# The second head's probabilities scaled on ScalarE instead of VectorE, in an attention loop of 128 steps

## What is computed

```python
def _gqa(q, k, v):
    scale = 1.0 / np.sqrt(q.shape[-1])
    scores = jnp.einsum('bsghd,btgd->bghst', q, k) * scale
    p = jax.nn.softmax(scores, axis=-1)
    return jnp.einsum('bghst,btgd->bsghd', p, v)
...
core = _gqa(q, k, v).reshape(b, s, nh * d)
qx = _fp8_linear_pertensor(ln_out, wqx, wqx_scale, qx_in_scale).reshape(b, s, g, hpg, d)
...
xout = _gqa(qx, kx, vx).reshape(b, s, nh * d)
cat = jnp.concatenate([core, xout], axis=-1)
catq = _div_clamp_fp8(cat, proj_smooth)
return jnp.einsum('bsi,oi->bso', catq, wproj) * (proj_in_scale * proj_w_scale)
```

## Time and profile before

| | |
|---|---|
| median of three runs | 1796.29 us (1796.28 to 1796.57) |
| profiled execution, its own time | 1798.47 us |
| its span | 1796.4 us |
| TensorE busy | 1741.4 us, 97% |
| VectorE busy | 1409.3 us, 78% |
| ScalarE busy | 1102.0 us, 61% |
| line 1244 (the scaling, 128x512) | 256 times, 124.5 us, 486 ns each |
| line 1002 (the exponential) | 256 times, 174.3 us, 689 ns each |

### The profile page before, as it was taken

How to read it: one execution, slowest core, us unless ns; L and a number is a source line. 1 busy time by engine, 2 the same in 40 slices (tenths; PEclk the granted TensorE clock), 3 DMA queues, 4 the chain that set the end, 5 groups by cost and what they waited for, 6 DMA issues and landing times.

```text
span 1796.4 us, 31332 instructions
## 1 busy us (share of the span) xinstructions
PE 1741.4 (97%) x10664; PEld 1186.5 (66%) x10664; DVE 1409.3 (78%) x4581; ACT 1102.0 (61%) x2378; POOL 272.0 (15%) x428
## 2 busy tenths in 40 slices
PE   9999999988999999999999999999999999989998
PEld 4444445666777776777777777777777777654554
DVE  1243526689888997888998889899889988979996
ACT  1131415376777775667677667777667766657776
POOL 0000000211111211111121111111112112201111
PEclk9999999999999999999999999999999999999999
DMA  7000000101312230121012012111210112000000
GB/s 270 24 0 24 0 0 25 37 1 52 105 48 85 71 95 3 55 73 36 26 48 73 24 50 73 36 36 39 75 41 19 61 54 95 3 1 19 24 24 30
DMA packets 45596, 83.30 MB, mean 46 GB/s; under 512 B 3584, under 2 KB 22528, under 8 KB 45056
## 3 DMA queue, kind: packets, MB, share of 16 engines
q1 hardware_dynamic: 45440, 81.31, 13.8%
HBM read 69.77 MB, written 10.49 MB: 45 GB/s over the span
## 4 chain that ended last, share of the span: by engine, by line
PE 68%; DVE 15%; issue 10%; ACT 4%; POOL 2%; DMA 0%; POOLq 0%; ACTq 0%
PE bank L536 15%; PE bank L645 8%; PE bank L599 7%; PE bank L694 6%; PE bank L623 4%; PE bank L730 3%; PE bank L410 3%; PE bank L496 3%; PE bank L470 3%; PE bank L458 3%; PE bank L488 3%; PE bank L578 3%; DVE nq L1234 2%; PE bank L437 2%; DVE nmx L1380 2%
## 5 line engine op out<-in xcount | busy, mean ns | idle before, releaser
L536 PE MATMUL bank<-wqs,XQ 128*128 128x256 f16 x2048 | 245.9, 274 | 4.6 <-DVE x L1265 4.6
L599 PE MATMUL bank<-prT,KV 128*128 128x256 f32 x1024 | 246.9, 384 | 0.0
L645 PE MATMUL bank<-kT,qT 128*128 128x512 f32 x512 | 242.2, 595 | 0.9 <-issue 0.9
L599 PEld LDWEIGHTS bank<-prT,KV 128*128 128x128 f32 x1024 | 190.5, 191 | 73.2 <-issue 52.2
L536 PEld LDWEIGHTS bank<-wqs,XQ 128*128 128x128 bf16 x2048 | 198.9, 99 | 43.6 <-DVE x L1265 11.4
L1002 ACT ACTIVATE pr<-bank,nmx 128x512 f32<-128x512 f32 x256 | 174.3, 689 | 42.7 <-DVE nmx L1380 41.4
L1549 POOL TENSOR_TENSOR rdev<-gvar,cst 128x7 f32<-128x7 f32 x128 | 191.0, 1492 | 10.0
L1547 POOL TENSOR_TENSOR gvar<-mvB,geps 128x7 f32<-128x7 f32 x128 | 30.8, 241 | 1061.4 <-DVE mvB L1224 1053.9
L1380 DVE TENSOR_REDUCE nmx<-bank 128x1 f32<-128x512 f32 x256 | 169.4, 683 | 12.0 <-PE bank L645 7.9
L694 PE MATMUL bank<-identf,pr 128*128 128x128 f32 x1024 | 153.7, 278 | 24.9 <-DVE pr L1244 20.1
L813 ACT ACTIVATE prT<-bank 128x512 f32<-128x512 f32 x256 | 153.2, 614 | 21.6 <-PE bank L694 21.4
(11 more groups left out here) (179 smaller groups left out, 3102.0 us busy)
## 6 DMA issues: line engine op xcount, KB each, us to landing
wa<-in_wgu SPq DMA_DIRECT2D x32, 512.0 KB, 3.7
wst<-in_wcat SPq DMA_DIRECT2D x21, 512.0 KB, 4.1
wpst<-in_wproj SPq DMA_DIRECT2D x8, 1024.0 KB, 6.4
wa<-in_wdn SPq DMA_DIRECT2D x16, 512.0 KB, 3.7
xT<-in_xT SPq DMA_DIRECT2D x4, 1024.0 KB, 6.9
wkx<-in_wkvx SPq DMA_DIRECT2D x8, 512.0 KB, 5.3
tern_gu<-wa SPq DMA_DIRECT2D x16, 256.0 KB, 2.0
wgu<-tern_gu SPq DMA_DIRECT2D x2, 2048.0 KB, 7.4
```

The costliest lines, as they stand in the source:

```text
L536: ins = mm(dst, XQ[:, b, c, k, j * P:(j + 1) * P], w, start=(k == 0 and m == 0), stop=(k == KT - 1 and m == 1))
L599: ins = mm(OB[:, 0:2 * P], KV[:, n % 2, t, P:2 * P], prT[:, st % 2, t, :, :].rearrange("p h s -> p (h s)"), start=(t == 0), stop=(t == ST ...
L645: mm(SB_[h][:], qT[:, h, st * P:(st + 1) * P], kT[:, :], start=True, stop=True).then_inc(s["scores_made"], 1)
```

## The change

In `scale_rows` VectorE takes both reciprocals, but multiplies only head 0. The second reciprocal signals a new semaphore, `ri_ready`; ScalarE waits for it and multiplies head 1 by it with an activation, in place, after `raw_kv` and `cross_out` and ahead of `ob_out`; it signals `pr1_scaled`, on which TensorE's turning of head 1 waits. The scaling of head 0 now comes after the wait for the second exponential and after the second reciprocal. The second reciprocal also waits until ScalarE's scaling of the step before is done, since that reads the same column of `ri`.

```diff
@@ TensorE, in pair
                     for h in range(2):
-                        pe.wait_ge(s["pr_scaled"], 2 * T + h + 1)
+                        pe.wait_ge(s["pr1_scaled" if h else "pr_scaled"], T + 1)
@@ ScalarE, in pair
                     if st == 1 and n > 1:
                         cross_out(n)
+                    act.wait_ge(s["ri_ready"], T + 1)
+                    act_f(pr[:, 1, :], pr[:, 1, :], ACT.Copy, scale=ri[:, 1:2]).then_inc(s["pr1_scaled"], 1)
                     if T:
                         ob_out(T - 1)
@@ VectorE
             def scale_rows(T, st):
 
-                for h in range(2):
-                    dve.wait_ge(s["exp_done"], 2 * T + h + 1)
-                    own.do(v.reciprocal(ri[:, h:h + 1], su[:, st, h:h + 1]))
-                    own.sync()
-                    v.tensor_scalar(pr[:, h, :], pr[:, h, :], ri[:, h:h + 1], None, ALU.mult).then_inc(s["pr_scaled"], 1)
+                dve.wait_ge(s["exp_done"], 2 * T + 1)
+                own.do(v.reciprocal(ri[:, 0:1], su[:, st, 0:1]))
+                dve.wait_ge(s["exp_done"], 2 * T + 2)
+                if T:
+                    dve.wait_ge(s["pr1_scaled"], T)
+                v.reciprocal(ri[:, 1:2], su[:, st, 1:2]).then_inc(s["ri_ready"], 1)
+                own.sync()
+                v.tensor_scalar(pr[:, 0, :], pr[:, 0, :], ri[:, 0:1], None, ALU.mult).then_inc(s["pr_scaled"], 1)
```

More of the change, by code:

```diff
@@ L222, in build @@
             max_ready exp_done raw_out kv_out kvx_out qt_out kt_out kxt_out ob_out pt_out pxt_out xexp_done
-            bn_ready stats_ready nq_ready pr_scaled xs_sub px_scaled cq_ready acc_done
+            bn_ready stats_ready nq_ready pr_scaled ri_ready pr1_scaled xs_sub px_scaled cq_ready acc_done
             wh_ready wl_ready wp_ready vx_copied cross_made cross_out
```

## The result

The changed kernel takes 1816.12 us (median of 4; 1815.76 to 1817.30), the kernel before in the same sitting 1796.43 us (1796.28 to 1798.17). The ratio is 1.0109, 95% interval 1.0091 to 1.0126: 19.7 us more. The forecast was 1815.7 us.

What follows compares the result with a forecast made beforehand. TensorE, 97% busy, bounds the kernel, losing time mainly at line 694 waiting for VectorE's scaling in first steps. Terms 9.2 + 1.3 + 3.5 + 5.4 = 19.4 us, added to the median, gave 1815.7 us; range 1803 to 1832.

Steps and rivals of the forecast that it cites:

- Kind A: 14 of 32 first steps, where exponentials are late: head 0 ready 0.66 us later with TensorE already waiting, 9.2 us.
- The last two steps: Last two steps of the loop, exponentials late too: head 0 ready 0.66 us later in each, 1.3 us.
- Second step: Second step of each pair: head 1, scaled on ScalarE, reaches TensorE 0.11 us late, 32 times, 3.5 us.
- Kind B: Other 18 first steps, exponentials ready and VectorE itself late: 0.3 us more each, 5.4 us.
- the carry: Rounding's net lateness from second to fourth steps into the next first step: 0.6 us, 0.2 after VectorE's waits for scores.
- my own sign of being wrong: Forecast fails if late first steps do not move, or second-step lateness reaches TensorE elsewhere than line 694.
- Rival 1: Fourth step's 0.43 us relief reaches first steps, 18 of which gain 0.33 us each: 1804.4 us, chance 0.14.
- rival 2: VectorE's relief reaches ScalarE's exponentials, which come 0.93 us earlier in 14 first steps: faster, 1783.5 us, chance 0.09.
- Rival 4: Over the whole loop, losses and relief cancel, with the second exponential hidden: 1796 us, chance 0.05.
- Rival 3: ScalarE's queue becomes the path, its added 0.63 us delaying the exponentials of 14 first steps: 1831.7 us, chance 0.12.

Runs made afterwards that it cites:

- e9_fourth_step: Against the kernel before, only the fourth step of each pair scales its second head on ScalarE, in the change's order: 1793.34 us, ratio 0.9981.
- e7_second_and_third: Against the kernel before, only the second and third steps of each pair scale their second head on ScalarE, in the change's order: 1813.77 us, ratio 1.0095.
- e1_reciprocals_first: Against the kernel before, VectorE takes both reciprocals first but still scales both heads; nothing moves to ScalarE: 1812.63 us, ratio 1.0079.
- e8_reciprocals_first_behind: Changed kernel with ScalarE's scaling behind the copy of the attended rows in first and third steps: 1813.46 us, ratio 1.0092 to the kernel before.

## Why the forecast held, point by point

*Kind A, 9.2 us.* Right in place and mechanism, a little too large. Here is the step of the earlier trace rows in the changed kernel, 7 us later:

```profile
956.16 0.16 DVE L1247 RECIPROCAL ri<-su 128x1 f32<-128x1 f32 x1 [0.50 <-ACT pr L1002]
956.24 0.47 DVE L1249 TENSOR_SCALAR pr<-pr,ri 128x512 f32<-128x512 f32 x1
956.36 0.72 ACT L1012 ACTIVATE pr<-pr,ri 128x512 f32<-128x512 f32 x1 [0.23 <-DVE ri L1247]
956.77 0.66 PE L694 MATMUL bank<-identf,pr 128*128 128x128 f32 x4 [2.01 <-DVE pr L1249]
956.99 0.61 ACT L979 ACTIVATE yb<-bank,rsT 128x128 bf16<-128x128 f32 x2
957.63 0.29 DVE L1256 TENSOR_SCALAR yb<-yb 128x512 bf16<-128x512 bf16 x1 [0.91 <-ACT yb L979]
```

VectorE idles 0.50 us for the second exponential, TensorE 2.01 us in place of 1.49. Eleven of the 13 steps cost 0.52 or 0.53 each and two 0.32 and 0.45, not 0.66: the scaling follows the second reciprocal by 0.08 us, since it waits only for the first. Sum 6.5 us. Line 694 starts 1.27 us after the first reciprocal; I had 1.4.

*The last two steps, 1.3 us.* The last but one costs 0.53 (in the table it is among the third steps), the last 1.11: 1.6 together, about right in size. Of the 1.11, 0.53 is what e9_fourth_step shows for this step, where only fourth steps have the new order; the other 0.58 is no part of my mechanism, since the last step takes 0.57 us more in e7_second_and_third too, where it is left as before; what makes it stays open.

*Second step, 3.5 us.* Right: 4.3 us. In a pair with even b (step 57):

```profile
930.58 1.27 ACT L987 ACTIVATE yb<-bank,rsT 128x512 bf16<-128x512 f32 x2
931.72 0.74 ACT L1012 ACTIVATE pr<-pr,ri 128x512 f32<-128x512 f32 x1
932.33 0.64 ACT L979 ACTIVATE yb<-bank,rsT 128x128 bf16<-128x128 f32 x2
```

```profile
931.42 0.63 PE L694 MATMUL bank<-identf,pr 128*128 128x128 f32 x4
931.88 0.60 PE L578 MATMUL bank<-identf,nq 128*128 128x128 f32 x4
932.51 0.66 PE L694 MATMUL bank<-identf,pr 128*128 128x128 f32 x4
```

Head 1 is scaled at 932.46 and turned at 932.51, where 0.44 us after line 578 would have been 932.32. It is 0.25 us a step with even b and 0.05 with odd b. The scaling holds the queue for 0.61 us (931.72 to 932.33; I had 0.63). The Trainium skill, page "ScalarE: Activation LUTs", section "What ACT_TABLE_LOAD costs", has figures that give 0.613 us as an estimate (706 ns less 93 ns of overlap), and the trace agrees. Rounding starts 3.58 us after the reciprocal; I had 3.7.

*Kind B, 5.4 us from the carry.* The size came out, the place did not. The delays of rounding were about right (+0.51, +0.44, and 2.03 us after the reciprocal in the fourth step, where I had 1.95), and I let them travel to the next first step, with a third of them lost in waits for scores. In the changed kernel they did not get there. The first instruction behind rounding that TensorE needs is the accumulation, and the fourth step's projections need it before. VectorE and TensorE of the changed kernel at step 55:

```profile
905.40 0.75 DVE L1270 SCALAR_TENSOR_TENSOR x<-bank,pscale,x 128x512 f32<-128x512 f32 x1
906.07 1.28 DVE L1385 TENSOR_REDUCE nmx<-bank 128x1 f32<-128x512 f32 x2
```

```profile
904.68 1.45 PE L645 MATMUL bank<-kT,qT 128*128 128x512 f32 x3
906.21 1.92 PE L536 MATMUL bank<-wqs,XQ 128*128 128x256 f16 x16
```

The accumulation ends at 906.15 and the projections begin at 906.21. Before, it ran from 898.97 to 899.72 and they began at 900.25, straight after the scores. There 5.4 us are lost, and kind B is 0.05 us shorter each. That my kind B gave 5.4 us too is chance. The failed step is the sentence that lateness is taken up by "VectorE's waits for scores"; I had looked for what VectorE waits for, and not for who waits for VectorE on the way. By my own sign of being wrong, "if lateness in the second step reaches TensorE in other places than line 694", the mechanism of this term is refuted: it reaches line 536, in the fourth step, once the third step's lateness is added (0.00 with the second step alone, 0.22 with both).

*Not in the sum at all:* the fall of the clock after a longer pause (1.67 us once in the trace), and 1.8 us in the first nine steps. So that 19.4 us came so near to 19.7 is in part luck: kind A was too large by 2.7 us, 5.4 us were put in the wrong place, and these two were missing.

*Two readings of the rows.* The 58.4 us of the earlier trace rows count one wait twice: all 18 waits on the matmul row are among the 37 on the weight-load row, at the same steps, and TensorE's matmuls stood 20.1 us for this reason, not 58. (On the two rows the changed kernel has 67.9 us for VectorE's scaling and 8.9 for ScalarE's; I had some 73.) And kind B is not all alike: in steps 0, 4 and 120 the weight load waits 3.97, 2.87 and 2.27 us, not 0.57 or less. Neither stands in the sum.

*The rivals.* Rival 1, the relief that carries, and rival 2, the relief that reaches the exponentials, both fall with the time of the changed kernel and with its kind B, 0.05 us shorter where they have 0.33 and 0.57. The run without the second scaling says the same of the relief: 3 us, where rival 1 has 5.9 (18 x 0.33) and rival 2 has 23 (14 x 0.93 and 18 x 0.57). Rival 4, in which losses and relief cancel, falls with the measured 1816 us. Rival 3, ScalarE's queue as the path of kind A, does not show in the change; a late ScalarE queue is what happened in the run with head 0 first, through line 863. The rule of the Trainium skill, page "ScalarE: Activation LUTs", section "Rules for kernel authors", that multiplications belong on VectorE, held in its result. Its reason, the engines' rates, explains at most the second step's 4.3 us: there head 1 is 0.25 us late, and an activation of 486 ns in place of 740 would by estimate have been in time (931.72 + 0.49 = 932.21, before 932.32). The other stretches hang on the order and on the place in the queue, and in the fourth step the slower engine cost nothing.

## What to carry to other kernels

An engine that is a third idle is not free at each place of its queue: a moved instruction delays all that stands behind it, and what counts is who waits for the next one. Follow a delay on an in-order engine instruction by instruction, and ask at each who reads its result; it comes to light at the first of them that has no slack, here the accumulation behind the rounding. And price the relief by itself, with the work left out, before moving anything: here 53 us of busy time were worth 3.

## What the runs showed of the hardware that I had not expected

A longer pause of TensorE can cost more than its length. At five places of the loop (steps 44, 60, 76, 92 and 108) it idles 1.48 to 1.50 us in the kernel before and in eight of the other runs (all but e1_reciprocals_first and e8_reciprocals_first_behind), and the granted clock stays at 2.4 GHz behind each of these 45 pauses. With pauses of 2.01 or 2.02 us (the changed kernel and e8_reciprocals_first_behind) it fell to 1.2 GHz behind three of ten, with 2.15 us (e1_reciprocals_first) behind three of five, and each fall cost 1.67 to 1.68 us. Which of the longer pauses it follows, these traces do not show. The mean granted clock goes with much of the spread between executions of one kernel: those of the kernel before at a mean clock of 0.994 took 1794.8 to 1797.1 us, those at 0.991 took 1800.1 to 1801.3.
